# Four transformer layers on one core: engine orders planned with other issue times, transfer times, a margin of 1.3 and other weights

## What is computed

```python
def layer0(x):                       # masked self-attention with rope, 77-token cross-attention, MLP
    x = x + g_msa * attn(modulate(ln(x)), mask) @ attn_out_W
    x = x + g_x * cross(modulate(ln(x)), cond_tokens) @ co_W
    return x + g_mlp * (gelu(modulate(ln(x)) @ mlp_W1 + b1) @ mlp_W2 + b2)
def layer1(x):                       # one cross-attention
    return x + (cross(adaln(x), adaln(ctx)) @ Wp + bp)
def layer2(x):                       # self-attention, cross-attention, MLP
    ...
def layer3(x):                       # self-attention with rope, cross-attention with rope, MLP
    ...
```

## Time and profile before

| | us |
|---|---|
| median of 3 runs | 2812.86 (2801.97 to 2818.2) |
| the profiled execution | 2808.65 |
| its span, first to last instruction | 2806.5 |
| TensorE (PE) busy | 2694.6 (96%) |
| VectorE (DVE) busy | 1821.8 (65%) |
| ScalarE (ACT) busy | 1442.5 (51%) |
| GpSimd (POOL) busy | 291.4 (10%) |
| mean granted TensorE clock | 0.977 of full speed |

### The profile page before, as it was taken

How to read it: one execution, slowest core, us unless ns; L and a number is a source line. 1 busy time by engine, 2 the same in 40 slices (tenths; PEclk the granted TensorE clock), 3 DMA queues, 4 the chain that set the end, 5 groups by cost and what they waited for, 6 DMA issues and landing times.

```text
span 2806.5 us, 57501 instructions
## 1 busy us (share of the span) xinstructions
PE 2694.6 (96%) x21118; PEld 1992.1 (71%) x21118; DVE 1821.8 (65%) x4675; ACT 1442.5 (51%) x2293; POOL 291.4 (10%) x346
## 2 busy tenths in 40 slices
PE   7989999999999999999999999999999999999998
PEld 5656777777776766666777777777776776776777
DVE  4576656755765367675667676676777667676652
ACT  1344554455454556454555555555555555556553
POOL 0000000000001111110111111111000000000000
PEclk9899999999999999998999999999999999999999
DMA  6434243333234365643433333333243332422410
GB/s 201 143 107 126 89 125 103 94 99 128 89 90 126 93 202 168 194 148 105 128 122 116 113 121 109 120 110 121 89 145 111 104 111 87 133 90 81 134 60 17
DMA packets 295964, 326.28 MB, mean 116 GB/s; under 512 B 85386, under 2 KB 186858, under 8 KB 295372
## 3 DMA queue, kind: packets, MB, share of 16 engines
q1 hardware_dynamic: 263244, 275.52, 32.3%
q10 hardware_dynamic: 32256, 47.07, 4.6%
q0 software_dynamic: 192, 0.01, 0.0%
HBM read 203.42 MB, written 118.31 MB: 115 GB/s over the span
## 4 chain that ended last, share of the span: by engine, by line
PE 75%; DVE 11%; DMA 5%; issue 3%; ACT 3%; SPq 2%; POOL 0%; ACTq 0%; DVEq 0%; POOLq 0%
PE gen L1329 12%; PE gen L1320 10%; PE gen L1195 10%; PE gen L1278 9%; PE gen L1161 9%; DVE row_max L1652 6%; PE score L1253 4%; PE score L1208 3%; PE score L1237 3%; PE gen L1289 3%; PE score L1223 3%; PE score L1259 3%; PE gen L1170 2%; PE gen L1300 2%; DMA max_scratch<-maxT 1%
## 5 line engine op out<-in xcount | busy, mean ns | idle before, releaser
L1652 DVE TENSOR_REDUCE row_max<-score 128x4 f32<-128x1024 f32 (+1 forms) x640 | 650.0, 1046 | 123.2 <-PE score L1237 104.4
L1469 ACT ACTIVATE probs<-score 128x1024 f32<-128x1024 f32 (+1 forms) x576 | 567.9, 1023 | 259.6 <-PE score L1253 151.8
L1320 PE MATMUL gen<-xnT,w_w1M 128*128 128x256 f32 x1536 | 361.9, 386 | 1.6 <-ACT xnT L1411 1.6
L1329 PE MATMUL gen<-w_w2M,hT 128*128 128x256 f32 x1536 | 352.3, 383 | 4.5 <-ACT hT L1495 4.4
L1505 POOL TENSOR_TENSOR rstd<-var_eps,minus_half 128x2 f32<-128x2 f32 x160 | 112.0, 700 | 2170.4 <-DVE var_eps L1548 2158.0
L1329 PEld LDWEIGHTS gen<-w_w2M,hT 128*128 128x128 f32 x1536 | 287.0, 191 | 51.5 <-issue 11.8
L1320 PEld LDWEIGHTS gen<-xnT,w_w1M 128*128 128x128 f32 x1536 | 283.7, 191 | 49.4 <-ACT xnT L1411 2.5
L1411 ACT ACTIVATE xnT<-gen,mod_all 128x256 f32<-128x256 f32 x288 | 146.9, 564 | 146.5 <-PE gen L1170 144.3
L1476 ACT COPY oT<-gen 128x512 f32<-128x512 f32 x224 | 131.8, 588 | 163.5 <-PE gen L1278 163.4
L1495 ACT ACTIVATE hT<-gen,b_b 128x256 f32<-128x256 f32 x384 | 157.7, 472 | 112.8 <-PE gen L1320 111.8
L1223 PE MATMUL score<-k_self,q_stack 64*128 64x256 f32 x1536 | 190.4, 340 | 21.3 <-DVE row_max L1652 17.5
(11 more groups left out here) (162 smaller groups left out, 4219.6 us busy)
## 6 DMA issues: line engine op xcount, KB each, us to landing
q_stack<-parts_scratch SPq DMA_DIRECT2D x336, 256.0 KB
parts_scratch<-parts ACTq DMA_DIRECT2D x160, 256.0 KB, 2.6
parts_scratch<-parts SPq DMA_DIRECT2D x160, 256.0 KB, 3.0
k_self<-parts_scratch SPq DMA_DIRECT2D x144, 256.0 KB, 3.7
k_cross<-parts_scratch SPq DMA_DIRECT2D x192, 78.0 KB, 2.5
x_scratch<-x SPq DMA_DIRECT2D x48, 256.0 KB, 3.4
x_in<-x_scratch SPq DMA_DIRECT2D x48, 256.0 KB, 2.8
gate<-gates_scratch SPq DMA_DIRECT2D x80, 128.0 KB, 3.4
```

The costliest lines, as they stand in the source:

```text
L1320: mm = pe.matmul(buf[:, i * S:i * S + S], w["M"]["w1"][:, fc, col:col + P], xnT[s][:, fc, :], start=fc == 0, stop=fc == FC - 1)
L1329: mm = pe.matmul(buf[:, 0:D], hT[:, j, c * P:c * P + P], w["M"]["w2"][:, j, :], start=j == 0, stop=j == FFC - 1)
L1469: act.activation(probs[st.probs][0:keys, :, :], score[st.fill.buf][0:keys, :, :].rearrange("p a (r q) -> p (a r) q", r=2), ACT.Exp, bias=k ...
L1652: dve.tensor_reduce(dst, src, AX_X, ALU.max).then_inc(max_done[b], 1)
```

## The change

No step is added or taken away, and no instruction of a step changes: the numbers by which the planner sets the order do. In words:

- Issue times on SP: `zq` 0.4 to 0.55, `sm` 0.4 to 0.56, `sd` 0.4 to 0.53, `lh` 1.26 to 1.27.
- Landing times: `zq` 2.2 to 2.6, `sm` and `sd` 2.2 to 2.7, `ph` 2.8 (context 2.5) to 2.6, `pw` 3.0 (2.6) to 2.6, `lh` 4.4 (3.2) to 3.9, `ll` 3.7 (2.6) to 3.3.
- All 14 kinds of transfers (`TRANSFERS`) are then counted 1.3 times as long, so `sm` and `sd` go from 2.2 to 3.51, `lh` from 4.4 (3.2) to 5.07, `ll` from 3.7 (2.6) to 4.29, `ldx` from 2.8 to 3.64.
- A job's age counts 14 for each job instead of 12, and keeping the tiling counts 6 instead of 4.

```diff
--- before.py
+++ after.py
@@ -102,7 +102,9 @@
 ENGINES = ("pe", "act", "dve", "pool", "sp")
 HOP = {"pe": 0.29, "act": 0.21, "dve": 0.14, "pool": 0.12, "sp": 0.1}
 TABLE = 1.28
-ISSUE = {"ldw": 2.5, "la": 0.5, "ms": 0.4, "zq": 0.4, "lh": 1.26, "ll": 0.63, "sm": 0.4, "sd": 0.4}
+TRANSFERS = ("ldx", "ldc", "ldg", "stx", "zq", "sm", "sd", "ldw", "ph", "pw", "lh", "ll", "la", "ms")
+MARGIN, AGE, STAY = 1.3, 14, 6
+ISSUE = {"ldw": 2.5, "la": 0.5, "ms": 0.4, "zq": 0.55, "lh": 1.27, "ll": 0.63, "sm": 0.56, "sd": 0.53}
 TILES = {"S": "rows", "ST": "rows", "W": "columns"}
 SWITCH = {("whole", "rows"): 0.095, ("rows", "whole"): 0.095, ("rows", "columns"): 0.095, ("columns", "rows"): 0.1,
           ("whole", "columns"): 0.09, ("columns", "whole"): 0.0}
@@ -117,14 +119,12 @@
         return (0.6 if blk.qkv_bias else 0.32) if context else 0.91 if blk.qkv_bias else 0.5
     if name == "lo":
         return (0.42 if blk.qkv_bias else 0.3) if context else 0.75 if blk.qkv_bias else 0.62
-    if name == "ph":
-        return 2.5 if context else 2.8
-    if name == "pw":
-        return 2.6 if context else 3.0
+    if name in ("ph", "pw"):
+        return 2.6
     if name == "lh":
-        return 3.2 if context else 4.4
+        return 3.9
     if name == "ll":
-        return 2.6 if context else 3.7
+        return 3.3
     if name == "qkv":
         return 0.9 if not whole and j else 1.73
     if name == "ve" and not whole:
@@ -140,7 +140,7 @@
             "ST": 0.34 + 0.43 * mask if whole else 0.3, "ex": 0.92, "W": 0.99 if whole else 0.56, "pv": 0.48,
             "oX": 0.44, "dv": 0.63, "atT": 0.22 if whole else 0.44, "ae": 0.26 if whole else 0.48, "out": 1.73,
             "up": 1.73, "ge": 0.73, "down": 3.45,
-            "ldx": 2.8, "ldc": 2.2, "ldg": 4.0, "stx": 2.2, "zq": 2.2, "sm": 2.2, "sd": 2.2, "ldw": 9.0,
+            "ldx": 2.8, "ldc": 2.2, "ldg": 4.0, "stx": 2.2, "zq": 2.6, "sm": 2.7, "sd": 2.7, "ldw": 9.0,
             "md": 3.5, "ma": 0.5, "mg": 1.0, "mh": 0.6, "ms": 2.6, "la": 5.0}[name]
 
 
@@ -151,7 +151,7 @@
         self.job, (self.li, self.seq), self.slot = job, JOBS[job], job % SLOTS
         self.k, self.blk, self.name, self.j, self.eng, self.fill = k, blk, name, j, eng, fill
         self.after = [a for a in after if a is not None]
-        self.before, self.cost = [], cost(blk, name, j)
+        self.before, self.cost = [], cost(blk, name, j) * (MARGIN if name in TRANSFERS else 1.0)
         self.takes, self.gives = rings_of(blk, name, j)
         self.buf = self.n = None
         self.early = False
@@ -431,7 +431,7 @@
                 can = [st for st in could[eng] if startable(st)]
                 if not can:
                     continue
-                st = min(can, key=lambda st: (12 * st.job - st.rank - 4 * (eng == "pe" and TILES.get(st.name, "whole") == self.tiles), 0))
+                st = min(can, key=lambda st: (AGE * st.job - st.rank - STAY * (eng == "pe" and TILES.get(st.name, "whole") == self.tiles), 0))
                 could[eng].remove(st)
                 self.order[eng].append(st)
                 started = True
```

## The result

The changed kernel takes 2793.5 us (median of 11 runs, 2783.66 to 2799.72) against 2812.86 before (11 runs, 2801.97 to 2818.2). The ratio is 0.9932, 95% interval 0.9918 to 0.9947, so it is faster by 0.7%, 19 us. The forecast was 2775. The profiled execution took 2783.66 us, span 2781.5, and is the fastest of the 11; the one of before took 2808.65.

A forecast was written before the change was run, and what follows sets the result against it. The prediction took PE, busy 96% of the span, as the bound. Its terms, -24 - 12 - 9 + 3 + 4 + 2 + 2 = -34, took 2808.65 to 2775 us, range 2755 to 2797.

The forecast's parts named there:

- first rival: L1: landing times long only by contention, later ST steps just as late, L1 term 0, time 2787; chance 0.13.
- L3: Layer L3: projections part the side-by-side scorings, fewer row_max waits and less lost clock; -24 us, bounds 0 and 30.
- the signs given beforehand: L3 windows: no 10 us at clock 0.51, idle near 1 us per 100; a row_max wait over 1 us refutes.
- L1: Layer L1: more PE work between S and ST covers the maxima's trip; -12 us, bounds 0 and 22 saved.
- Into L2: 1200 to 1400 us: fewer long rows of side-by-side scorings; -9 us, from 10 lost to 20 gained.
- the new x12 at job 32: Entry into L2: new x12 scoring row, two ST and an S behind it; counted against the gain, no separate size.
- Start and end: Start: 3 us gained on maxima, xT behind out costs more, net +3. End: last xT nearer its out, +4.
- The bare xT: Start: job 0's xT directly behind its out, PE waits 4.3 us, plus 1.7 of clock if it drops.
- ACT: Short ST-to-W distances under 2.2 us rise from 10 to 33, 0.1 us for each of the 23: +2 us.
- That rival: PE waits for ACT where W follows ST too soon and a table load falls between: 2828 us; chance 0.12.
- PE's busy time: Sign: falls with the clock's part only, to about 2665; staying at 2695 with clock 0.977 would make the forecast wrong.

The follow-up runs named there:

- e5: Changed kernel with margin 1.0, age 12 and tiling 4, so only the new issue and landing times stay: 2822.5 us, ratio 1.0044.
- e6: Kernel before, same order, self-attention maximum in L2 and L3 taken over the first half of the keys only: 2792.7 us, ratio 0.9929.
- e2: The change's numbers for steps of layer L1 alone, the numbers of the kernel before elsewhere: 2795.3 us, ratio 0.9947.
- e10: The change's numbers for steps of L1, L2 and L3, the numbers of the kernel before in L0: 2768.8 us, ratio 0.9849.

## Why the prediction was right, and where not

The time lies in the forecast's range of 2755 to 2797, near its upper end, and is nearer to the first rival's 2787 than to 2775. Of the two large terms one came as forecast and one mostly did not.

*L3, right in mechanism and nearly in size.* -24 forecast, -23 found, with 8.3 of idle time (12.5 counted before rounding down) and 14.7 of clock (as counted). e1, e5 and e6 bear the mechanism out. Of the signs given beforehand, the half clock did go; idle time is 1.7 us in each 100, not near 1; and one wait for row_max of 1.10 us is left at 2294, though over 1 us was to refute the term. That bound was drawn too tight: no stretch of half clock follows this wait.

*L1, the term that failed.* -12 forecast, 0 found by the table's row, and 4 to 6 us by the means over all executions with the two orders: half of the term or less. The step said that with more work between S and ST the maxima's trip is covered. That part came true: those waits are gone. What the step left out is that other transfers are late in L1 as well, the stores to parts_scratch first of all, and that PE met some of these next. The chain of waits in L1 of the changed kernel:

```profile
978.97 7.30 DMA parts_scratch<-parts
...
987.59 4.73 DMA q_stack<-parts_scratch
...
994.57 1.93 PE score L1237 x16
```
```profile
991.09 1.30 SPq L1056 DMA_DIRECT2D k_cross<-parts_scratch  x1
```

A store to parts_scratch takes 7.30 us, planned as 2.6 x 1.3 = 3.4, and SP's queue, which works strictly in order, stands behind it until 986.3. The loads that it issues then stay inside their plan (4.73 for the one shown, 5.07 planned), but start late. The chain has no name for the last 2.25 us before 994.57; the trace has the load of k_cross's low part, issued at 991.09 and landed after 3.39 us at 994.48. PE is idle for 2.96 us. A second place, ACT and PE:

```profile
1172.06 0.84 ACT L1459 ACTIVATE parts<-gen,b_qk 128x256 fp32r<-128x256 f32 x2 [3.40 <-DMA parts_scratch<-parts]
```
```profile
1173.42 1.11 PE L1289 MATMUL gen<-ident,oT 128*128 128x128 f32 x4 [2.59 <-ACT oT L1476]
```

ACT stands 3.40 us for the parts buffer, which a store of 5.15 us has not left yet, and the copy to oT behind it in ACT's list makes PE wait 2.59 us. A third, at 904, is 0.95 us. These places are 6.5 of the 14 us idle before 1190; the rest are short waits, for ACT's xnT above all (2.6 us in 4), and that they too come from transfers is not shown. With a DMA share of 0.53 both kernels have about 17 us idle from 900 to 1200.

The Trainium skill (DMA: Bandwidth & Descriptors, Latency and other measured facts) says that access to HBM goes from 0.2 us on average to 2 us at high load. The trace agrees only in part. Stores of 256 KB to parts_scratch, issued by ACT and SP, landed in the changed kernel after medians of 3.6 and 3.7 us in L1, at a DMA share of 0.53, and after 2.2 and 2.7 from 1400 to 2100, at 0.38. But in L1 before, at the same 0.53, it was 2.7 and 2.8, and those of 78 KB took 4.7 and 4.5 in the changed kernel from 200 to 900, at 0.35. So the mean share does not give the time of a store, and what made the one above take 7.30 is open. The first rival's sentence (transfers are slow by contention) may be true of L1, but its mechanism is not what happened, since ST is not late. e2 shows that the same numbers can gain 15 us behind another order of L0, and there the slowest store in L1 took 5.2 us; my bounds of 0 and 22 held.

*Into L2.* -9 forecast, -12 found, but the new x12 at job 32 cost what was feared, 1.67, 0.63, 0.34 and 0.42 us of waits before 1195 and a clock at half from 1192 on, and its waits stand in L1's row. With them, 5 to 6 us are left.

*Start and end.* +3 and +4 forecast, +5 and +5 found. At the start the waits for the maxima went, as counted; the load hT<-in_adaln3b, which landed after 7.8 us instead of 4.5 and for which PE waits 5.2, was in no term. The bare xT shows as PE's timeline rows:

```profile
121.10 1.12 PE L1170 MATMUL gen<-ident,xhat 128*128 128x128 f32 x4 [4.91 <-DVE xhat L1554]
```
```profile
2714.32 1.11 PE L1170 MATMUL gen<-ident,xhat 128*128 128x128 f32 x4 [1.22 <-DVE xhat L1554]
```

4.91 us where 4.3 was worked out, with the clock at half for 6.8 us about it. At the end it is 1.22, where 4.3 - 1.4 = 2.9 had been counted; 1.54 us of waiting for a load to q_stack stand just ahead of it, and 6.8 us of half clock follow.

*200 to 900.* 0 forecast, -5 found: the order of L0 had some 20 waits of 0.2 to 0.7 us for row_max before, and after a 2.57 and a 0.51 at its very start (job 1's cross-attention) has seven, of 0.16 to 0.55.

*ACT* did not become what PE waits for: the matmuls' waits for probs fall from 10.3 to 5.3 us over all lines. Those of the weight loads (the products with V) rise from 1.0 to 6.8 us, 15 times with at most 0.8, which run beside matmuls in part. That rival was wrong here, and the +2 counted for ACT is not to be seen as a term of its own.

*PE's busy time* fell to 2685.7, not to 2665: the clock gave 12 us, not 30, since L1 and the start kept their stretches at half speed.

Of the 34 us, by the rows of the table (L1's with the blur told above), the L1 term is 12 too many; the unforeseen 5 of L0 and 3 at L2 make up part, and that they fell this way is luck, since no term said so. Small ones take the rest, and 25 are left: 2808.65 - 25 = 2783.66, the profiled execution. The remaining 10 us to the median are the spread among executions, 16 us from end to end, of which the profiled one is the fast end. This spread goes with the granted clock: the three fastest of the 11 had means of 0.981 to 0.983, the three slowest 0.977 to 0.979, and 0.004 of 2790 us is 11 us. Why the same order is granted more clock in one execution than in another is not shown.

## What to carry to other kernels

When a fixed order is drawn by a greedy planner (one that always takes the best step at hand), its constants are a set: a margin on transfers lengthens ranks, so the age that is weighed against them has to grow too. Here each half alone cost 93 and 242 us, and both together gained 19. Read a planned order before running it: count instructions that share two buffers and stand side by side, and steps with nothing between them and their producer; then look which transfer is slowest where traffic is heaviest, since covering one trip can only show the next. And try new planner numbers by stage, with a run for each mixture: the version with the old numbers in L0 (e10) runs in 2768.8 us, 1.5% below before, but the one with new numbers in L3 alone (e1) in 2835.9.

## What the runs showed of the chip that I had not expected

Waits can cost clock as well, and not by their length alone. In the profiled executions e10 has more idle time than the change (100 against 96 us) and is 11 us faster, since its clock loses 33 us instead of 53; e5 has less idle time than before (105 against 112) and is slower, with 90 us of clock instead of 65. In e6 three waits of together 1.4 us at 2157 to 2160 were still followed by 6.8 us at 1.2 GHz, while in before a single wait of 2.20 us that ended at 893 was followed by none. For a kernel that keeps PE busy 96% of the time, a wait is to be judged by what the granted clock does behind it, not by its length alone.
